# Four places instead of one for the turned row scales in an attention pipeline

## The reference

```python
scores = jnp.einsum('bqhd,bkhd->bhqk', q_full, k_full) * softmax_scale
scores = jnp.where(causal[None, None], scores, jnp.finfo(scores.dtype).min)
attn = jax.nn.softmax(scores, axis=-1)
out = jnp.einsum('bhqk,bkhd->bqhd', attn, v).reshape(B, S, H * VD)
```

## Time and profile before

| what | value |
|---|---|
| median of the runs | 2024.18 us |
| the profiled execution, its own time | 2021.53 us |
| its span | 2019.5 us |
| mean granted TensorE clock | 0.965 |
| busy: PE, DVE, ACT, POOL | 91%, 60%, 49%, 43% |

### The profile page before, as it was taken

How to read it: one execution, slowest core, us unless ns; L and a number is a source line. 1 busy time by engine, 2 the same in 40 slices (tenths; PEclk the granted TensorE clock), 3 DMA queues, 4 the chain that set the end, 5 groups by cost and what they waited for, 6 DMA issues and landing times. The chain is left out here.

```text
span 2019.5 us, 44379 instructions
## 1 busy us (share of the span) xinstructions
PE 1839.7 (91%) x15472; PEld 1438.7 (71%) x15472; DVE 1221.3 (60%) x2653; ACT 992.3 (49%) x2135; POOL 870.3 (43%) x641
## 2 busy tenths in 40 slices
PE   6999878699999999999999999998499999978999
PEld 4678677576777767676676766776388888867887
DVE  5555266487878878787887888878431111115543
ACT  2211055487877877787877878777321001003110
POOL 2221110366768677676867768675000000004311
PEclk9999989899999999999999999999799999989999
DMA  6442142302112121211212121221552322324421
GB/s 230 169 149 94 72 133 78 89 21 79 61 68 65 48 80 48 80 46 66 71 57 77 35 80 65 64 65 54 171 190 88 113 90 83 104 95 145 141 88 63
DMA packets 111695, 182.45 MB, mean 90 GB/s; under 512 B 27472, under 2 KB 64464, under 8 KB 109584
## 3 DMA queue, kind: packets, MB, share of 16 engines
q1 hardware_dynamic: 111632, 181.61, 27.6%
HBM read 122.06 MB, written 59.51 MB: 90 GB/s over the span
## 5 line engine op out<-in xcount | busy, mean ns | idle before, releaser
L940 PE MATMUL psS<-keyT,q 128*128 128x512 f32 (+2 forms) x2304 | 483.7, 356 | 59.7 <-POOL q L1145 48.3
L940 PEld LDWEIGHTS psS<-keyT,q 128*128 128x128 f32 x2304 | 390.7, 194 | 156.2 <-DVE negmax L1071 46.9
L1021 ACT ACTIVATE prob<-prob,negmax 128x640 f32<-128x640 f32 (+7 forms) x512 | 392.0, 767 | 152.8 <-DVE negmax L1071 150.4
L1081 DVE STREAM_TRANSPOSE pT<-prob 128x640 f32<-128x640 f32 (+7 forms) x512 | 375.8, 758 | 51.5 <-PE psV L957 47.1
L1071 DVE CUSTOM_DVE_ANT_0 prob<-psS,mask 128x640 f32<-128x640 f32 (+7 forms) x512 | 370.9, 741 | 45.7 <-PE psS L940 35.0
L413 PE MATMUL f_psy<-f_weff,f_xT 128*128 128x512 f32 x1344 | 313.8, 393 | 0.0
L1136 POOL TENSOR_TENSOR pT<-pT,cosT 64x512 f32<-64x512 f32 x128 | 164.7, 1286 | 331.6 <-ACT pT L1006 318.9
L1307 PE MATMUL o_psy<-o_w,o_o 128*128 128x512 f32 x1344 | 304.8, 389 | 0.0
L1307 PEld LDWEIGHTS o_psy<-o_w,o_o 128*128 128x128 f32 x1344 | 252.3, 188 | 52.4
L413 PEld LDWEIGHTS f_psy<-f_weff,f_xT 128*128 128x128 f32 x1344 | 250.9, 188 | 53.9 <-issue 1.7
L957 PE MATMUL psV<-pT,val 32*64 32x512 f32 (+3 forms) x8192 | 265.7, 408 | 6.2 <-DVE pT L1081 6.2
(11 more groups left out here) (99 smaller groups left out, 1875.1 us busy)
## 6 DMA issues: line engine op xcount, KB each, us to landing
wo<-in_wo SPq DMA_DIRECT2D x16, 1024.0 KB, 5.7
pT<-row_scales SPq DMA_DIRECT2D x128, 128.0 KB, 2.8
oT<-pT SPq DMA_DIRECT2D x64, 256.0 KB, 2.4
o_in<-oT SPq DMA_DIRECT2D x32, 512.0 KB, 5.2
f_xt<-in_x SPq DMA_DIRECT2D x16, 512.0 KB, 4.2
f_w_in<-in_w SPq DMA_DIRECT2D x16, 512.0 KB, 6.1
w_sum<-f_w_in SPq DMA_DIRECT2D x16, 512.0 KB, 5.1
x<-f_xo SPq DMA_DIRECT2D x16, 512.0 KB, 2.7
```

The source lines that it names most:

```text
L940: ins = nc.tensor.matmul(psS[:, slot, start + x0:start + x1], q[:, e, a, t * P:(t + 1) * P], k.keyT[:, m, b * S + x0:b * S + x1], start=(i ...
L1021: nc.scalar.activation(row, row, ACT.Exp, bias=negmax[:, n % 8:n % 8 + 1], scale=-1.0, accum_out=rowsum[:, column(n, s):column(n, s) + 1]) ...
L1081: nc.vector.transpose(pT[:, n % 2, t, 0:width], prob[:, n % RING, 0:width]).then_inc(turned, 1)
```

## The change

`rinvT` gets four places of 32 columns. The place of a unit is `x // QT`, which is 0 to 3 and comes round every two steps. The transpose of a unit writes its own place, and waits for the stores of the unit four before it instead of one before it. The stores read the place of their unit. Nothing is added to the work or to the transfers.

```diff
-        rinvT = c.sb("rinvT", [P, 32])
+        rinvT = c.sb("rinvT", [P, 4, 32])
...
-                    sp.dma_start(rows[:, 32 * g:32 * g + 32], rinvT[32 * g + x:32 * g + x + QT, :]).then_inc(r_stored, 16)
+                    sp.dma_start(rows[:, 32 * g:32 * g + 32], rinvT[32 * g + x:32 * g + x + QT, x // QT, :]).then_inc(r_stored, 16)
...
-                if later(number, 1):
-                    dve.wait_ge(r_stored, number * 64)
-                nc.vector.transpose(rinvT[:], rinv[:]).then_inc(r_turned, 1)
+                if later(number, 4):
+                    dve.wait_ge(r_stored, number * 64 - 192)
+                nc.vector.transpose(rinvT[:, x // QT, :], rinv[:]).then_inc(r_turned, 1)
```

## The result

The changed kernel takes 1963.73 us (median of 4 runs, 1960.9 to 1964.91) against 2023.56 (median of 4 runs) for the kernel before on the same chip. The ratio is 0.9697, with a 95% interval of 0.9684 to 0.971: 3.0% faster. The profiled execution took 1964.07 us, 57.5 less than the one of before.

What follows compares the result with a forecast made beforehand. TensorE was the bound, idle before S8 and F0 in the wake of DVE's R stalls. Idle time 31.0, last step 0.8 and clock 12.5 sum to 44.3 us off 2021.53: 1977.2, as median 1980; range 1968 to 1998.

Steps and rivals of the forecast that it cites:

- The chain from R1 to S8: Even steps: R1's stall gone, M6 about 4.0 us after V0, B2 about 7, then GpSimd releases S8.
- the limit set for it: The forecast is wrong if GpSimd's chain comes later than 7 us after V0.
- rival (b): GpSimd doesn't hold S8 up, TensorE packs closer: down to 60.5 a pair, gain 57, 1966 to 1974 us; chance 0.14.
- Two smaller signs: F0 waits 0.3 to 0.5 us; GpSimd's idle time at L1136 unchanged but for about 2 us less in even steps.
- the floor of 61.16 us for a pair of steps: GpSimd's loop, 31.28 us over an odd step and 29.88 over an even one, as the shortest possible pair.
- the 29.78 us "at full clock without idle time" of an even step: TensorE's even step at full clock, 32.01 less the 2.23 us idle before S8.
- before S8 of even steps: TensorE's idle time before S8 in even steps: some 24 us of the 31 gained.
- odd steps, F0 and S8: TensorE's idle time before F0 and S8 in odd steps: some 7 us of the 31 gained.
- lowered clock: 13 steps with clock below 1.00 cost 16.7 us; three quarters, 12.5 us, taken to come back.
- last step: One stall of R0 on the path where V waits 6.2 us for DVE: 0.8 us gained.
- Both stalls go: R0's and R1's waits for stores before the transpose into `rinvT` vanish, up to 105.3 us of DVE time.
- rival (c): Wait handed on to DVE before T1, T2 or O0; gain 5 to 20 us, time 2004 to 2019; chance 0.10.

Runs made afterwards that it cites:

- the dose experiment: Changed kernel with extra DVE transposes behind R1 in each step: 4 of them (1.33 us) took 1963.24 us, 8 (2.69 us) took 2011.06 us.
- the two GpSimd experiments: Changed kernel with A3's sine product on 64 of 512 columns, 1954.78 us; changed kernel with cosine products waiting only for ScalarE's first copy, 1953.99 us.

## Why the prediction was right and wrong

The chain from R1 to S8 held at every link. The 105.3 us of idle DVE time went whole and brought 58 us; T2 waits 0.55 us for V1, M6 starts 3.95 us after V0 (4.0 forecast), B2 at 7.16 (about 7, and 7 was also the limit set for it), GpSimd releases S8, and the dose experiment shows the slack behind R1 between 1.33 and 2.69 us, 0.9 us of the larger dose coming out at S8. That is a slack of about 1.8.

The number that came is that of rival (b), 60.49 us a pair where it said 60.5, with the clock full; but its mechanism didn't come, and the match is luck. It had GpSimd no longer hold S8 up and the waits before S8 and S9 vanish; they stand at 0.36 and 0.25 us in the even steps, both for GpSimd. Where they vanish from the even steps, with GpSimd's loop shortened, an even and an odd step take 59.98 together, less than (b) said. Two smaller signs failed as well: F0 waits 0.24 us (0.3 to 0.5 forecast), and the idle time of GpSimd before L1136 fell in even steps by 0.8 us a step (0.3 at full clock), not by 2; at full clock it was the 1.9 us before B2 that went, down to 0.15.

The step that failed is the floor of 61.16 us for a pair of steps. The loop is real in the even steps, as the two GpSimd experiments show, but I read its length off stretches that held waits of their own. B2 to A0 was taken as 7.54 us in an even and, within the 31.28, 8.94 in an odd step; after the change it is 1075.02 - 1067.71 = 7.31 and 8.58. The part of the loop that runs through TensorE, ScalarE and O0 of DVE was still late by 0.2 to 0.4 us from R0's stall: with R0 alone freed it takes 7.30 and 8.63 us (means at full clock), with R1 alone freed 9.19 and 9.28.

The same mistake sits in the 29.78 us "at full clock without idle time" of an even step. After the change it is 29.52 - 0.36 = 29.16. With R0 alone freed, whose even steps keep their long wait before S8, the full-clock ones have 31.34 - 2.17 = 29.17 as well. So the 0.6 us came from R0's stall of 1.1 us (its mean in even steps), for which the prediction had a term in odd steps only. DVE ran from there without a gap to M1; in the step of 1034.92 TensorE's way from S8 to the end of S4 was 0.2 us longer than after the change, and S5 waited 0.4 for M1. The earlier trace rows left out the waits for M, 7.1 us in the same view, of which 3.2 lie in the eight even steps at full clock, 2.4 in the odd steps at lowered clock and 1.5 in the last step.

Term by term, for the 30 steps:

| term | forecast | measured |
|---|---|---|
| before S8 of even steps | 24 | 15 x (2.00 - 0.36) = 24.6 |
| odd steps, F0 and S8 | 7 | 8.6 - 0.6 = 8.0 |
| small waits of even steps for DVE | 0 | 15 x (29.78 - 29.16) = 9.3 |
| lowered clock | 12.5 | the rest of 57.8: 15.9 |
| last step | 0.8 | -0.2 |

In the prediction's own terms the 13 missing us are: the floor, 15 x (61.16 - 60.49) = 10.1; the clock, all of the 16.7 us instead of 12.5, so 4.2; less 1.0 in the last step. That all of the 16.7 came back is what the rule of the Trainium skill named above had, which I gave as the time 4 us shorter. The table's last row but one is a rest and not measured by itself, and its border with the row above isn't sharp: in the seven even steps with the lowered clock there was no wait before S5, and freeing R0 alone left them as they were (30.7 us and the wait before S8, 30.6 before). So 8 x 0.6 = 5 of the 9.3 us belong to R0's stall alone, and the rest came only together with the clock. What is shown is that none of the 30 steps had the lowered clock after the change, and that it returned with the added work. What idle pattern brings it is open: with R0 freed the odd steps lost it and the even ones kept it, behind 2 us before S8; with R1 freed four even steps had it, around the wait before Q0, and the odd ones none in spite of 0.63 us before F0.

Two statements on the way were too simple. "Both stalls go" was true, but not that each was the cause of its own part: R1's stall shielded R0's, and freeing it alone brought 0.3%. And rival (c), the stall handed on, came near what half of this change does, by another path: from R1 to R0 through SyncE, not to T1, T2 or O0 for V and ScalarE.

## What to carry to other kernels

Two users of one buffer can share one stall. Freeing the earlier one alone handed its wait to the later one (0.3% gained), freeing the later one alone gave 1.1%, both 3%; so count the gain for the pair and free both. Before adding a buffer look at what stands ahead of the late transfer on its queue; here moving the loads in SyncE's order did as much as three more places. And when a path's length is read off a trace in which the stall is still there, any stretch that passes through the stalled engine holds some of it: take a base from the steps with the least stall, with all the small waits listed, and give the floor a lower end.

## What was not expected of the hardware

The regularity: once no step waits for a landing, 15 even steps agree within 0.14 us and 15 odd ones within 0.12, where they had scattered over 2.2 and 4.5 us. Part of that scatter was the lowered clock: one odd step of before took 35.38 us, and in the kernel with 2.69 us of added work five odd steps at lowered clock took (494.8 - 10 x 31.96) / 5 = 35.0 us against 31.96 at full clock, so in a step that loses the clock, an idle time that is itself 0.9 us longer costs another 3.
